# A decoder kernel on one core: where VectorE rounds the last kinds of quantised tokens, and when slot 4's values are projected

## The reference

```python
ln_out = _ln(hidden_states, ln_w, ln_b)
q = _ln(_fp8_linear_pertensor(ln_out, wq, wq_scale, q_in_scale).reshape(b, s, g, hpg, d), qln_w, qln_b)
k = _ln(_fp8_linear_pertensor(ln_out, wk, wk_scale, k_in_scale).reshape(b, s, g, d), kln_w, kln_b)
v = _fp8_linear_pertensor(ln_out, wv, wv_scale, v_in_scale).reshape(b, s, g, d)
core = _gqa(q, k, v).reshape(b, s, nh * d)
qx = _ln(_fp8_linear_pertensor(ln_out, wqx, ...), qxln_w, qxln_b)
kx, vx = jnp.split(jnp.einsum('bsi,oi->bso', cond, w_kv_x), 2, axis=-1)
xout = _gqa(qx, _ln(kx), vx).reshape(b, s, nh * d)
catq = _div_clamp_fp8(jnp.concatenate([core, xout], axis=-1), proj_smooth)
x = x + jnp.einsum('bsi,oi->bso', catq, wproj) * (proj_in_scale * proj_w_scale)
```

## Time and profile before

| | us |
|---|---|
| median of 3 runs | 960.12 (960.01 to 960.75) |
| the profiled execution | 960.35 |
| its span, first to last instruction | 958.6 |
| TensorE busy | 877.6 (92%) |
| VectorE busy | 707.4 (74%) |
| ScalarE busy | 563.6 (59%) |
| GpSimd busy | 133.3 (14%) |
| mean granted clock of TensorE | 0.973 |

### The profile page before, as it was taken

One profiled execution on the slowest core, in us unless ns is written; L12 is line 12 of the kernel. 1 busy time (PEld: TensorE's weight loads), 2 busy tenths in 40 slices (PEclk: granted clock), 3 DMA queues, 4 the chain that ended last, 5 costly groups with the idle time before them and its releaser, 6 DMA issues.

```text
span 958.6 us, 15310 instructions
## 1 busy us (share of the span) xinstructions
PE 877.6 (92%) x4998; PEld 653.0 (68%) x4998; DVE 707.4 (74%) x1557; ACT 563.6 (59%) x2045; POOL 133.3 (14%) x186
## 2 busy tenths in 40 slices
PE   5989999999888789999999999999999988699796
PEld 3647566656667567878877787878787866455453
DVE  3673554556786888988989898899888988756643
ACT  3452235556565857777877687878777856331310
POOL 3001200100103112121212121212112211000000
PEclk9999999899999989999999999999999999899997
DMA  7001000000101132333333432423322622210000
GB/s 226 1 0 55 1 1 1 2 1 23 35 1 56 53 81 58 90 97 75 103 92 85 110 79 73 116 63 95 102 62 61 201 66 70 58 31 0 23 0 23
DMA packets 63953, 56.77 MB, mean 59 GB/s; under 512 B 11073, under 2 KB 62850, under 8 KB 63874
## 3 DMA queue, kind: packets, MB, share of 16 engines
q1 hardware_dynamic: 63776, 55.76, 21.4%
q10 hardware_dynamic: 98, 0.03, 0.0%
HBM read 21.15 MB, written 1.05 MB: 23 GB/s over the span
## 4 chain that ended last, share of the span: by engine, by line
PE 67%; DVE 20%; issue 5%; ACT 4%; SPq 3%; DMA 1%; POOL 1%; DVEq 0%
PE ps L933 10%; PE ps L946 8%; PE ps L878 7%; PE ps L1018 5%; PE ps L961 5%; PE ps L903 4%; SPq L580 3%; PE ps L920 3%; PE ps L730 3%; PE ps L720 2%; PE ps L743 2%; DVE group_probs L1754 2%; PE ps L841 2%; PE ps L708 2%; PE ps L782 2%
## 5 line engine op out<-in xcount | busy, mean ns | idle before, releaser
L1329 ACT ACTIVATE group_probs<-ps,score_bias 128x256 f32<-128x256 f32 x256 | 117.1, 484 | 54.3 <-DVE score_bias L1743 54.3
L1743 DVE TENSOR_REDUCE score_bias<-ps 128x2 f32<-128x512 f32 x128 | 87.7, 691 | 48.7 <-PE ps L946 48.5
L946 PE MATMUL ps<-group_kT,group_qT 128*128 128x256 f32 x512 | 116.0, 380 | 0.5 <-ACT group_qT L1295 0.5
L946 PEld LDWEIGHTS ps<-group_kT,group_qT 128*128 128x128 f32 x512 | 97.2, 190 | 26.9 <-issue 9.3
L1276 ACT ACTIVATE group_squares<-ps 128x128 f32<-128x128 f32 x384 | 105.2, 343 | 10.5 <-PE ps L878 9.2
L1276 ACT ACTIVATION_READ_ACCUMULATOR group_squares<-ps 128x1 f32 x384 | 97.3, 277 | 0.0
L1317 ACT ACTIVATE group_cat_y<-ps,vec_inv 128x256 bf16<-128x256 f32 x128 | 53.6, 470 | 67.4 <-PE ps L933 67.4
L2091 POOL TENSOR_TENSOR head_rstd<-head_sum,minus_half 128x7 f32<-128x7 f32 (+1 forms) x64 | 85.7, 1340 | 5.3
L878 PE MATMUL ps<-group_w_hi,xq 128*128 128x256 f32 x256 | 75.0, 320 | 4.1 <-DVE group_heads L1723 4.1
L961 PE MATMUL ps<-group_wp_hi,group_cat 128*128 128x256 f32 x256 | 70.0, 310 | 4.7 <-DVE group_cat L116 4.7
L1754 DVE TENSOR_SCALAR group_probs<-group_probs,score_inv 128x256 f32<-128x256 f32 x256 | 72.7, 347 | 0.5
(11 more groups left out here) (279 smaller groups left out, 1992.0 us busy)
## 6 DMA issues: line engine op xcount, KB each, us to landing
second<-laid SPq DMA_DIRECT2D x256, 64.0 KB, 2.1
group_probsT<-front_quant SPq DMA_DIRECT2D x240, 64.0 KB, 2.0
group_raw_p<-in_L_xattn_wproj_dram SPq DMA_DIRECT2D x16, 256.0 KB, 3.3
group_raw_w<-in_L_xattn_wq_dram SPq DMA_DIRECT2D x8, 256.0 KB, 2.9
group_raw_w<-in_L_xattn_wqx_dram SPq DMA_DIRECT2D x8, 256.0 KB, 3.1
group_raw_w<-in_L_xattn_w_kv_x_dram SPq DMA_DIRECT2D x16, 128.0 KB, 3.1
x_all<-in_x_dram SPq DMA_DIRECT2D x2, 512.0 KB, 6.2
front_work<-in_ctx_dram SPq DMA_DIRECT2D x1, 1024.0 KB, 7.0
```

The costliest lines, as they stand in the source:

```text
L946: last = pe.matmul(c.ps[:, bank, t * S:(t + 1) * S], c.qT[:, side, h, t * P:(t + 1) * P], c.kT[:, side, :], start=True, stop=True)
L1329: last = act.activation(c.probs[:, side, h, t, :], c.ps[:, fills.bank(name), t * S:(t + 1) * S], ACT.Exp, bias=c.score_bias[:, i:i + 1], a ...
L1743: v.tensor_reduce(c.score_bias[:, i:i + 2], c.ps[:, bank, :].rearrange("p (t n) -> p t n", n=S), AX.X, ALU.max, negate=True).then_inc(nega ...
```

## The change

It has two parts.

1. On VectorE, in slot 2 the order behind the transposes was: clamp and round n = 1, maxima, normalise. It becomes: normalise, maxima, clamp and round n = 1. In slot 3 it was: normalise, clamp and round n = 3, maxima. It becomes: normalise, maxima, clamp and round n = 3. Slot 1 has that order already.
2. In slot 4 (o.n == 4) TensorE projects the values of both token halves at the end of t = 1, and ScalarE copies them out (L1285) behind the copy of `values_x` of t = 1.

```diff
-                    def product(bank, at, kind):
+                    def product(bank, at, kind, t=t):
...
-                    if o.leads and t == 1:
-                        pair_values()
+                    if o.leads and t == 1 and o.n != 4:
+                        pair_values(1)
...
-                    if o.leads and t == 0:
-                        pair_values()
+                    if o.leads and t == 0 and o.n != 4:
+                        pair_values(0)
+                    if t == 1 and o.n == 4:
+                        pair_values(0)
+                        pair_values(1)
...
-                    if o.leads and t == 1:
+                    if o.leads and t == 1 and o.n != 4:
+                        take_pair_values()
                     bank, last = square_heads(1, 0, 3)
                     act.activation(c.values_x[:, o.n % 4, t, :], ...).then_inc(proj_read, 1)
+                    if t == 1 and o.n == 4:
+                        take_pair_values()
...
-                    if o.n == 2:
-                        clamp(1, 1)
-                        round_kind(1, 1)
+                    if o.projects:
+                        normalise_item(o)
+                    if o.scores:
                         item_max(o, 0)
                         item_max(o, 1)
-                    if o.projects:
-                        normalise_item(o)
-                    if o.n == 3:
-                        clamp(1, 3)
-                        round_kind(1, 3)
-                    if o.scores and o.n != 2:
-                        item_max(o, 0)
-                        item_max(o, 1)
-                    if o.n == 1:
-                        clamp(1, 0)
-                        round_kind(1, 0)
+                    kind = {1: 0, 2: 1, 3: 3}.get(o.n)
+                    if kind is not None:
+                        clamp(1, kind)
+                        round_kind(1, kind)
```

More of the change, by code:

```diff
@@ L880, in product, with pair_values @@
                         return last
-                    def pair_values():
+                    def pair_values(t):
                         name = ("Z", o.n)
                         bank = fills.bank(name) if t else fills.claim(pe, name)
-                        last = product(bank, t * W_WIDTH, 3)
+                        last = product(bank, t * W_WIDTH, 3, t)
                         if t:
@@ L1278, in square_heads, with take_pair_values @@
                         return bank, last
-                    bank, last = square_heads(0, 3, 4 if o.leads else 2)
-                    last.then_inc(proj_read, 1)
-                    if o.leads and t == 1:
+                    def take_pair_values():
                         name = ("Z", o.n)
@@ L1286, in take_projection @@
                                                    ACT.Copy), name)
+                    bank, last = square_heads(0, 3, 4 if o.leads else 2)
+                    last.then_inc(proj_read, 1)
+                    if o.leads and t == 1 and o.n != 4:
+                        take_pair_values()
                     bank, last = square_heads(1, 0, 3)
                     act.activation(c.values_x[:, o.n % 4, t, :], c.ps[:, bank, 3 * HD:4 * HD], ACT.Copy).then_inc(proj_read, 1)
+                    if t == 1 and o.n == 4:
+                        take_pair_values()
                 def take_item_heads(o):
```

## The result

| | before | with the change |
|---|---|---|
| median, 20 runs of each | 960.79 (958.14 to 965.53) | 964.14 (962.18 to 967.89) |
| ratio | | 1.0038 (95% interval 1.0022 to 1.0054) |
| the profiled execution, its span | 960.35, 958.6 | 967.39, 965.6 |
| mean granted clock | 0.973 | 0.967 |

By the ratio the change makes the kernel slower by 3.6 us (2.1 to 5.2); the two medians differ by 3.35. The forecast was 1.2 us slower, with a range up to 963.0; the measured 964.14 lies outside.

What follows compares the result with a forecast made beforehand. TensorE bounds from slot 4's output product on, whose start VectorE's cat_ready sets. That start moves from 359.27 to 360.5, +1.2 us; 960.35 becomes 961.55, and with the runs' median 0.23 lower, 961.3 us; range 959.9 to 963.0.

Steps and rivals of the forecast that it cites:

- the sum: Slot 4's output product on TensorE (L961) starts at 360.5 instead of 359.27: +1.2 us.
- The scaling on ScalarE held by the later rounding: Slot 2: L1248 waits for the second kind's rounding, starting at 334.87 instead of 330.60; L1709 follows 2.3 us later.
- the half clock in slot 3: Slot 3's weight transposes and heads run at half speed after the 6 us gap, yet cost nothing.
- The cover of the moves in slot 4: Moves of item 1's probabilities land at 362.7, the averaging needing them starts no earlier than 363.9: 1.2 us of cover.
- the clock behind L961: TensorE behind slot 4's output product: no slow stretch was expected there, so nothing was added.
- the scattered ones: TensorE's 2.4 us of idle time scattered over 317.5 to 322.0 before the change, after which the clock stayed at 1.00.
- a rival at 0.22: Gaps near 357 and 360 make TensorE's clock fall behind L961 for 3.4 us: +1.6 us, 962.9; chance 0.22.
- the slow stretch of before: TensorE at clock 0.50 from 354.6 to 358.0; said to be worth nothing, as L961 now waits for VectorE.
- the base: Time before the change: profiled execution 960.35 us, with the median of the runs 0.23 below it.
- the stated range: Whole-kernel time from 959.9 (nothing moves) to 963.0 (slow clock behind L961).
- The chance for slower: Whole kernel past the 962.0 bound: 0.07 from the forecast's spread and 0.20 from the slow clock, together 0.27.

Runs made afterwards that it cites:

- the experiments that took the hold away: The change with slot 2's old VectorE order (1.0005), with ScalarE's fourth-kind scaling moved to slot 3 (1.0006), or with slot 2's rounding put first (one execution, no ratio).
- The second profile: The changed kernel unaltered, profiled again with more runs against the kernel before: ratio 1.0015 (0.9994 to 1.0036).
- the five others with a gap there: The change with slot 2's order undone, 1.0005; scaling moved, 1.0006; that plus early third-kind rounding, 0.9961; rounding first in slot 2; and the values' move alone on the kernel before.
- the repeated measurement: More runs and a second profile of the unaltered changed kernel against the kernel before: ratio 1.0015 (0.9994 to 1.0036).

## Why the prediction was wrong

**Right: the sum.** The scaling on ScalarE held by the later rounding, the exponentials behind it, L1709's counterpart 2.3 us later (14.41 - 12.06 = 2.35), cat_ready 1.5 us later (34.28 - 32.84 = 1.44), the output product 1.2 us later (1.15): each came as written, and the experiments that took the hold away moved D by what it says. The remark held too that the half clock in slot 3 costs nothing: VectorE's maxima there started at 355.16, straight behind its normalising and without a wait for the scores. The second profile shows it again: there the half clock ended 14.2 us after the transpose, in the first 18.7 us after it, and D is 34.33 in both. The cover of the moves in slot 4 held as well.

**Wrong: the clock behind L961.** The step that failed is the one that begins "The change has gaps of about 1.0 us (before the values) and 1.5 us (before L961) in 4.7 us, which is nearest to the scattered ones, so I take no slow stretch". The slow stretch came, in both profiles of the change and in the five others with a gap there, at a cost of 1.2 to 1.9 us. It was a rival at 0.22, priced at +1.6 us, 962.9, and should have been the forecast. Two things stood behind the choice. First a miscount: the values are two products of four matmuls each, thus eight instructions and not sixteen. They end 1.2 us after they start, so the gap ahead of L961 is one piece of 2.0 us and not 1.5. The end of TensorE's values and that of VectorE's quantising both hang on the fourth kind, so the gap has this length in every version in which the values wait for it. The other gap of the forecast, 1.0 us ahead of the values, isn't needed for the fall: the second profile of the change has it (1.28 us), but in the first the half clock in slot 3 lasted until 348.6, TensorE came to the values only as the fourth kind was there, and the clock fell behind the 2.04 us alone. Second, the wrong neighbour: in the stretch of 317.5 to 322.0, 2.4 us of idle time in all, the longest piece was 1.57 us, and the single gap of 2.47 us near 304 in the same trace, which the prediction didn't use, was followed by 3.3 us at 0.50. TensorE there, and its clock behind the gap, before:

```profile
321.89 1.31 PE L920 MATMUL ps<-ident,group_heads 128*128 128x128 f32 x8 [1.57 <-DVE group_wp_lo L1709]
306.34 0.70 PE L920 MATMUL ps<-ident,group_heads 128*128 128x128 f32 x4 [2.47 <-DVE group_w_lo L1704]
```

```profile
306.80:310.10 3.30, 3.30 (x18) 0.50 0.00 0
```

The gap of 2.47 us was the nearer one. The long gap of 6.20 us cost nothing, as it lay where VectorE was the late engine, and the short one cost 1.2 us, as TensorE was the late engine from there on. The Trainium skill's advice against long idle gaps ("TensorE: Matmul & The Clock Gate", section "Why this matters for your kernels") had been tied to the gap of 6.20 us, and the trace agrees with it there: 0.50 over 341.0 to 348.6. It speaks of longer gaps than the 2.03 and 2.47 us after which the clock fell here, so the measured rows decide, and the page alone would not have given the slow stretch behind L961.

**What the change really moved.** Before, TensorE's gap of 3.37 us lay inside slot 4's projection, and the slow stretch behind it fell on matmuls that were in the shadow of VectorE's quantising: it ended 0.34 us late. With the values at the end, the waiting moved to the last place before TensorE becomes the late engine, and the slow stretch moved with it into the open. The prediction noted that "the slow stretch of before is worth nothing here", but didn't ask where it would go.

**Wrong in part: the range and the base.** The three runs known beforehand, 960.12, lie a little low against 960.79 over 20, which is 0.7 us of the 2.8 that were missed. The clock's fall is 1.2 to 1.5; by itself it would have left the time inside the stated range (962.5 to 962.8), and only with the base does it come out above it, at 963.2 to 963.4. What is left, 0.7 to 0.9 us, is within the interval; its cause stays open, and the repeated measurement doesn't show it. The chance for slower was 0.27 and should have been well over one half: D alone brought 1.2 of the 1.9 us that can be told from no change, so any one further microsecond decided.

## What to carry to other kernels

Before a step is put behind another on an engine, look for who waits for it and what is queued behind that waiter: here one scaled copy on ScalarE held eight exponentials that were ready, and moving that copy, with VectorE's order left as in the change, was worth 3.8 us in D. When waiting is moved along TensorE's program, expect the slow stretch to move with it, and ask which engine is late there: a gap in the shadow of another engine was free here, and a shorter one at the point where TensorE becomes the late engine cost the slow stretch behind it. Measure a local edit in the trace between two anchors close around it; 20 runs of each gave it to 1.5 us here, two rows of one profile to some 0.6.

## What the runs showed of the hardware

- A gap of 2.01 to 3.15 us right ahead of the dense part went with a fall to half clock in seven profiles of seven. The fall came between 2.2 us before the gap's end and 1.5 us after it, and 2.8 to 4.6 us behind the gap ran at 0.50. In the two profiles with 16 matmuls without use in the gap (1.9 us) the clock stayed at 1.00.
- The same program has a slow stretch near 80 us in some executions and not in others (0.50 against 1.00 over 80.0 to 83.4). It lasted from near 79 to near 86 us in the first profile of the change and was worth 3.3 us against the first of before; in the second profile of the change it was about half as long.
- A `pe.matmul` of 256 columns on float32 tiles shows in the trace as two matmuls of 0.21 us each, at a granted clock of 1.00 (32 for 16 in the code, 357.88 to 364.60); on the rounded type as one of 0.12 to 0.13.
